# The first batch's first stage gets a program of its own

## The reference, cut to what matters

```
x  = x + quant(layernorm(x)) @ quant(ctx).T      # first block
x  = x + ffn(layernorm(x))                       # second block
ffn(h): q, k, v projections of rmsnorm(h); 16 query heads, 4 key/value heads of 128, rmsnorm of q and k, RoPE,
        causal softmax, values, output projection, residual; then rmsnorm, top 2 of 8 experts, their products, residual
```

## Time and profile before

| | |
|---|---|
| median of three runs | 1615.73 us (1614.37 to 1616.39) |
| the profiled execution's own time | 1621.27 us |
| its span in the trace | 1619.5 us |
| PE busy in the span | 1352.6 us (84%) |
| DVE, ACT, POOL busy | 766.7, 660.1, 381.9 us |
| mean granted TensorE clock | 0.93 of full speed |

### The profile page before, as it was taken

The page is one execution under the profiler, slowest core; times in us unless marked ns, Lnnn a source line. Parts: engine busy times, 40 slices in busy tenths (PEclk is TensorE's granted clock), DMA queues, the critical chain, the costliest instruction groups (busy, mean ns, idle before and its releaser), DMA issues. The chain is left out here.

```text
span 1619.5 us, 20299 instructions
## 1 busy us (share of the span) xinstructions
PE 1352.6 (84%) x6414; PEld 981.7 (61%) x6414; DVE 766.7 (47%) x2295; ACT 660.1 (41%) x2153; POOL 381.9 (24%) x558
## 2 busy tenths in 40 slices
PE   0467788899889998989999899999872599999996
PEld 0245566677667667767667777777651265665663
DVE  5626766555766555477565544554525211111110
ACT  3425664444645445465544544544520022222221
POOL 1021221213222222222223223223100123333332
PEclk9978798999989999999999999999995599999998
DMA  2223122434053131324212132330136523333332
GB/s 91 94 101 118 39 100 90 147 147 182 8 185 92 62 131 53 132 95 114 78 53 104 66 143 79 84 126 23 50 96 281 230 52 66 66 65 66 65 66 39
DMA packets 42440, 156.93 MB, mean 97 GB/s; under 512 B 5024, under 2 KB 5792, under 8 KB 33120
## 3 DMA queue, kind: packets, MB, share of 16 engines
q1 hardware_dynamic: 30624, 130.52, 21.5%
q0 software_dynamic: 10848, 24.65, 8.8%
q10 hardware_dynamic: 864, 0.46, 0.1%
HBM read 111.57 MB, written 44.04 MB: 96 GB/s over the span
## 5 line engine op out<-in xcount | busy, mean ns | idle before, releaser
L1032 DVE TENSOR_SCALAR_CACHE_REDUCE prob<-bank,nscale 128x128 f32<-128x128 f32 (+3 forms) x256 | 135.2, 547 | 296.0 <-PE bank L547 295.7
L403 POOL TENSOR_TENSOR prob<-prob,rtotal 128x128 f32<-128x128 f32 (+2 forms) x192 | 119.0, 629 | 433.9 <-DVE rtotal L1038 414.6
L760 ACT ACTIVATE pT<-bank 128x512 f32<-128x512 f32 (+3 forms) x256 | 104.5, 433 | 278.7 <-PE bank L555 278.3
L754 ACT ACTIVATE prob<-prob,bias 128x128 f32<-128x128 f32 (+3 forms) x256 | 144.9, 566 | 164.0 <-DVE prob L1032 163.0
L513 PE MATMUL bank<-w_hi,hT_hi 128*128 128x512 f32 (+1 forms) x512 | 191.9, 375 | 5.7 <-DVE rot L1006 4.3
L1396 PE MATMUL gu<-we,xT 128*128 x624 | 194.3, 465 | 2.3 <-ACT xT L1440 1.3
L384 POOL TENSOR_TENSOR r<-r,rot 128x640 f32<-128x640 f32 x64 | 103.4, 1616 | 368.0 <-DVE rot L1006 368.0
L566 PE MATMUL bank<-pT,v 128*128 128x512 f32 (+3 forms) x512 | 178.4, 451 | 1.4 <-ACT pT L760 1.4
L513 PE MATMUL bank<-w_lo,hT_hi 128*128 128x512 f32 (+1 forms) x512 | 178.4, 348 | 0.0
L513 PE MATMUL bank<-w_hi,hT_lo 128*128 128x512 f32 (+1 forms) x512 | 178.2, 348 | 0.0
L1396 PEld LDWEIGHTS gu<-we,xT 128*128 128x128 f32 x624 | 117.1, 193 | 62.1 <-issue 5.4
(11 more groups left out here) (226 smaller groups left out, 2523.5 us busy)
## 6 DMA issues: line engine op xcount, KB each, us to landing
w_hi<-ws_scratch SPq DMA_DIRECT2D x24, 1024.0 KB, 5.0
w_lo<-ws_scratch SPq DMA_DIRECT2D x24, 1024.0 KB, 7.3
we<-in_wexp SPq DMA_DIRECT2D x8, 2176.0 KB, 28.0
stage<-in_wqkvo SPq DMA_DIRECT2D x40, 256.0 KB, 6.3
ws_scratch<-w_hi SPq DMA_DIRECT2D x8, 1024.0 KB, 4.0
ws_scratch<-w_lo SPq DMA_DIRECT2D x8, 1024.0 KB, 7.0
w_hi<-ws_scratch SPq DMA_DIRECT2D x12, 512.0 KB, 6.1
w_lo<-ws_scratch SPq DMA_DIRECT2D x12, 512.0 KB, 7.0
```

The lines of the kernel that those rows point to most:

```text
L403: nc.gpsimd.tensor_tensor(p, p, rtotal[:, 4 * h + q:4 * h + q + 1].broadcast_to([P, KEYS[q]]), ALU.mult).then_inc(prob_ready, 1)
L754: nc.scalar.activation(p, p, ACT.Exp, bias=bias[:, 4 * h + q:4 * h + q + 1], scale=-1.0, accum_out=total[:, 4 * h + q:4 * h + q + 1]).then ...
L760: nc.scalar.activation(pT[:, PT_AT[j]:PT_AT[j] + QS[j]], bank[PT + j % 2][:, 0:QS[j]], ACT.Copy).then_inc(pt_copied, 1)
L1032: nc.vector.tensor_scalar(prob[h % 2][:, P_AT[q]:P_AT[q] + KEYS[q]], bank[SC + q % 2][:, 0:KEYS[q]], nscale[it % 2][:, q, h:h + 1], None, ...
```

## The change

The prologue gets its own operations; batches 1 to 3 keep theirs. Its core, with the functions added:

```
+ first_rows = [xw[0][:, :], xw[1][:, :], prob[0][:, 0:D], prob[0][:, D:2 * D]]      # four row tiles
+ amax_all, ainv_all, ascale_all: [P, TT, KC];  cmx: [NB, 1];  cmb: [NB, P]
+ FIRST_T, FIRST_P = (PT, PT + 1, AUX, PV), (0, 1, SC, SC + 1)                        # banks of transposes, of products
+ def wqkv(j, i): return aT[i] if j == 0 else w[i]                                    # group 0's q, k, v weights in aT
+ def q_bank(j, t): return bank[0] if j else bank[(0, SC)[t % 2]]
+ def kv_bank(j, t): return bank[1] if j else bank[(1, SC + 1)[t % 2]]
# DVE
+ def first_scales():            # maximum, reciprocal, two products for all four row tiles at once
+ def first_row_maxima(t): ...   # as in row_scales, into amax_all
+ def first_ctx_maxima(k):       # one 128x512 chunk of the context, waits for that chunk alone
+ def first_spread():
+     dve.wait_ge(cm_turned, 1)
+     nc.vector.tensor_reduce(cmx[:, :], bank[PV][0:NB, 0:P], AX.X, ALU.max).then_inc(cm_row, 1)
+     dve.wait_ge(cm_row, 1)
+     nc.vector.tensor_copy(cmb[:, :], cmx[:, :].broadcast_to([NB, P])).then_inc(cm_spread, 1)
+ def first_norms():             # nine steps on DVE in place of POOL's newton(0)
# PE
+ def first_maxima():
+     pe.wait_ge(camax_done, KC)
+     nc.tensor.transpose(bank[PV][0:NB, 0:P], camax[:, :], ident[:, :]).then_inc(cm_turned, 1)
+     pe.wait_ge(cm_spread, 1)
+     nc.tensor.transpose(bank[PV][:, P:P + NB], cmb[:, :], ident[0:NB, 0:NB]).then_inc(cm_back, 1)
+ def first_products():
+     for k in range(KC):
+         pe.wait_ge(cd_ready, k + 1)
+         for t in range(TT):
+             last = nc.tensor.matmul(bank[FIRST_P[t]][:, :], r[:, t, k * P:(k + 1) * P], cb[:, k, :], start=(k == 0), stop=(k == KC - 1))
# POOL
+ def add_first(t): ...          # the q part (512 wide) of add_rope(0, t); add_rope(0, t) keeps the k part (128 wide)
  tables():  + pool.wait_ge(cr_ready, KC)
- column_maxima(0)
- newton(0)
# SP
  save_x1(f): one DMA for each of four tiles, each as soon as its tile is summed (was one of 1 MB after the fourth)
  order: load_raw 0..5, save_x1(0), load_raw 6..11, load_x(1), load_ctx(1), save_qkv(0)
  (was:  load_raw 0..5, save_x1(0), load_x(1), load_ctx(1), save_qkv(0), load_raw 6..11)
```

More of the change, by code:

```diff
@@ L328, in _ @@
             save_x1(0)
+            for n in range(QKV, 2 * QKV):
+                load_raw(n)
             load_x(1)
@@ L458, in transposes_x @@
                 for k in range(KC):
-                    last = nc.tensor.transpose(bank[AUX][:, k * P:(k + 1) * P], xw[t % 2][:, k * P:(k + 1) * P], ident[:, :])
+                    last = nc.tensor.transpose(tr_bank(f, t)[:, k * P:(k + 1) * P], (xw[t % 2] if f else first_rows[t])[:, k * P:(k + 1) * P], ident[:, :])
                 last.then_inc(xt_done, 1)
@@ L668, in dequantise_rows @@
                 act.wait_ge(xr_ready, TT * f + t + 1)
+                row, back = (xw[t % 2], ascale[t % 2]) if f else (first_rows[t], ascale_all[:, t, :])
                 for k in range(KC):
                     sl = slice(k * P, (k + 1) * P)
-                    last = nc.scalar.activation(xw[t % 2][:, sl], xw[t % 2][:, sl], ACT.Copy, scale=ascale[t % 2][:, k:k + 1])
+                    last = nc.scalar.activation(row[:, sl], row[:, sl], ACT.Copy, scale=back[:, k:k + 1])
                 last.then_inc(xd_ready, 1)
@@ L736, in square_q @@
                 act.wait_ge(projq, TT * j + t + 1)
-                need(act, rope_added, TT * j + t - 1)
+                if j:
+                    act.wait_ge(rope_added, TT * j + t - 1)
+                else:
+                    need(act, first_added, t - 1)
                 for h in range(G):
-                    last = nc.scalar.activation(rot[t % 2][:, h * HD:(h + 1) * HD], bank[0][:, h * HD:(h + 1) * HD], ACT.Square,
+                    last = nc.scalar.activation(rot[t % 2][:, h * HD:(h + 1) * HD], q_bank(j, t)[:, h * HD:(h + 1) * HD], ACT.Square,
                                                 accum_out=ssum[:, t, h:h + 1])
@@ L1081, in _ @@
             sum_norm(0)
-            hidden_norm(0)
-            for c in range(RING_W, QKV):
-                lo_qkv(0, c)
+            lo_qkv(0, 3)
             for t in range(TT):
                 lo_h(0, t)
+            hidden_norm(0)
+            lo_qkv(0, 4)
+            lo_qkv(0, 5)
             dve.wait_ge(table_step, 11)
@@ L1089, in _ @@
                 rotate(0, t, False)
+                lo_qkv(1, t)
+            for t in range(TT):
                 rest_kv(0, t)
             start_norms(0)
+            first_norms()
             apply_norms(0)
@@ L1094, in _ @@
                 lo_qk(0, i)
-            for c in range(QKV):
-                lo_qkv(1, c)
+            lo_qkv(1, 4)
+            lo_qkv(1, 5)
             for it in range(NIT):
```

252 lines of the change are left out of this document (152 added, 100 removed).

## The result

The changed kernel takes 1579.95 us (median of four runs, 1578.85 to 1582.6) against 1616.06 us for the kernel before, ratio 0.978 with an interval of 0.9763 to 0.9797: 36.1 us less. Timed a second time, in five rounds on one chip, it took 1580.80 against 1617.45, ratio 0.977 (0.9754 to 0.9786). The forecast was 1575, with a range of 1567 to 1585.

The account below looks back on a forecast made before the run. Ahead of 131.5 us waits, not PE's list, were taken to set the pace; behind it PE's list does. The prologue's steps sum to -40.9 us, from 1615.7 to about 1575, range 1567 to 1585.

Parts of the forecast that it names:

- less: Rival: weight-ring loads delay the prologue, or iteration 0 pays some 6 us more for its all-reduce; 1577 to 1583, chance 0.25.
- Step A: Context scales at the program's start: column maxima without waiting for POOL's reduction, so DVE's first rounding moves from 30.65 to 20.5.
- Step B: Scaling and rounding of the context: ACT ends last, first chunk ready at 37.9, first product about 38 instead of 51.1.
- Step C: Context products and sum: sixteen matmuls take 9.0 us, statistics of the sum end at 51.2 instead of 72.2.
- D: Second norm and save of the sum: `hidden` begins at 54.2 instead of 76.8, without waiting for the save.
- G: From normalised k to iteration 0: two weight splits remain instead of six; first maxima at 90.6 instead of 131.5.
- E: Transposes after the second norm, in four banks: projections begin at 59.4 instead of 88.8, rounds take 5.2 instead of 12.0.
- Step F: Projections until k is normalised: two banks spare PE the wait for each rotation; k ready at 83.9 instead of 119.6.
- More: Rival: PE stays at full clock into iteration 0, of which 0.5 to 2.5 us passes on; 1573, chance 0.2.
- Slower: Rival: the first write to `aT` waits for late weight saves; 1625 if they land 90 us late, chance 0.02.
- My last sign of being wrong: The forecast would be wrong if first maxima to the end of attention took longer than 1092 us.

## Why the prediction was right, and where its sizes were off

**Where the bound is.** Right. What was gained lies ahead of iteration 0, and nothing behind it gives back or adds in a way that two traces of each kernel could show. The medians, 1579.95 and 1580.80, lie in the range of 1567 to 1585, but not in the band of the forecast itself (1573.5 to 1577): they lie in that of *less* (1577 to 1583), whose mechanism did not occur.

**Step A.** 20.5 forecast, 19.05 measured. Of the 1.45, 0.8 is luck: the input landed earlier, so the norm stood ready at 11.5 and not at 12.2. The four unknown operations with their waits and `ctx_scales` took 1.7 us (17.37 to 19.05, with the first transpose hidden beside the last maximum), 1.8 estimated; but 18.2 and 1.8 make 20.0, and I had written 20.5. The price that I read there as the worth of PE's maxima was that of the all-reduce's place.

**Step B.** ACT ends last, as said, so the step is counted from ACT's start: 18.3 us to the first product (17.42 to 35.72), 19.7 forecast. DVE's rounding is off the path by the slack I had named: in the variant with the all-reduce behind the tables ACT hid 1.8 us of its delay (2.5 named).

**Step C is the mis-sized term.** I took "x8" in the earlier trace rows as eight matmuls; it is four, since each product of 128x512 in f32 stands in the trace as two instructions, and the block shows x32 for sixteen. Read rightly, a first row tile at 5.32 and three at 3.70 give 16.4, where the block measured 15.9; the forecast's 9.0 us held half the work. PE's last product was to end at 46.9 and ended at 51.6, 4.7 late: 6.9 of the term, less the 2.2 that steps A and B were early. The last statistics were 3.2 late (54.4 for 51.2), since DVE's tail behind PE was 2.8 and not 4.3: in a block twice as long, the first bank is complete earlier before its end. And PE, not the arrival of the chunks, is the limit of this stretch.

**Steps D to G.** From there the distances are those of the forecast, with the forecast's in brackets: C to D 3.0 (3.0), D to E 4.2 (5.2), E to F 24.5 (24.5), F to G 6.7 (6.7). Step F holds inside as well: the first rotation comes 5.6 us after the first projection (5.6), q of tile 2 7.1 (7.0), the last q matmul 12.6 (12.7). Taken away again, three parts cost what was expected for them: transposes 6.0, splits 4.45, Newton 1.5. Two did not: the save 0.6 for 1.5, the second banks 18.6 for 12. From the first projection to the first maxima the change gained 11.6 us (42.75 before, 31.20 now), less than the banks alone cost when removed; so these prices hold in the new order and do not add up to the gain.

**The median.** The landmarks give 38.7 and 39.4 us, the medians 36.1 and 36.7. The forecast's own sum, 40.9, was 2.2 over the first of the landmarks: 3.2 late at C, and 1.0 back between D and E. The intervals of the two ratios stand for gains of 32.8 to 38.3 us and 34.6 to 39.8. The other 2 to 3 us are smaller than what the stretch behind the prologue does by itself (6.7 us between two executions of one kernel), but they came out alike in both timings. Whether a part of it belongs to the change stays open: the mean of that stretch is 1092.1 in two traces of before and 1093.3 in twelve with a changed prologue, which two traces can't decide.

**Rivals.** *More* needed PE to stay at full clock into iteration 0. The granted clock there was 1.00 (92.8 to 97 us), where before had 0.50 in its like stretch (131.5 to 136). PE's timeline:

```profile
93.37 0.41 PE L590 MATMUL bank<-kT_hi,qT_hi 128*128 128x384 f32 x1 [1.65 <-DVE prob L1119]
```

It waited 1.65 us here instead of 7.40, and this matmul took 0.41 instead of 0.66. But iteration 0 was as long as before to 0.04 us. That fits the all-reduce holding what follows; yet iteration 0 of before was itself 1.0 us shorter in its second trace, so a gain under 1 us would not be seen. *Less* did not happen: `stage` never held ACT between the squares. *Slower* was far off; its 1625 was also a slip, since saves that land 90 us late would give 1665 by its own rule. My last sign of being wrong, a stretch longer than 1092 us, was drawn from a window cut 2.9 us too early, and with 6.7 us of variation it could not have told anything: the second trace of the changed kernel has 1095.1.

## What to carry to other kernels

Where each engine waits for the tile before, give a prologue its own buffers and PSUM banks, and look at the order with them: one bank each for q and for k and v took 30.2 us in the kernel before, where the two alternated, and 42.4 with all q tiles first, against 23.9 with two banks each. A third of the last difference was clock: with waits of 2.7 us ahead of the q tiles the granted clock was 0.74, with two banks 0.93. Count instructions in a trace against those in the kernel before pricing them: x8 was four matmuls here. Before replacing a slow operation on another engine, move it to the front of that engine's list: an all-reduce that held DVE 10 us cost nothing once it stood ahead of independent work. And measure such a change at a landmark of the trace, since here the rest of the program varied by 6.7 us, more than most of the effects that were asked about.

## What was not expected of the hardware

- Two executions of one program differ by 6.7 us in some 1092 us of attention. For the same 5060 matmul instructions PE was busy 971.3 us at a mean clock of 0.94 in one and 962.0 at 0.95 in the other, while DVE, ACT and POOL differ by 0.6 at most. It is not that alone: over the fourteen traces the length does not follow PE's busy time (1090.8 us at 968.4 busy, 1095.0 at 965.4).
- The same 32 matmul instructions in the same order took 15.57 to 16.91 us in nine traces, by when their pace doubled, while the clock in the windows read 1.00 throughout.
- Each all-reduce of the kernel before comes with two instructions on POOL's sequencer that change its configuration, eight for four calls, and each call has its own wait of 5.81 to 6.37 us. With the all-reduce first in POOL's list the first such instruction stands at 1.0 us, and the call ran 0.14 us behind its input. By the view of line 374:

```profile
L374 POOLq MODIFY_POOL_CONFIG  x8: 11/11/16, 23.5 to 694.2; - x8
L374 POOL PARTITION_ALL_REDUCE camaxall<-camax x4: 391/392/392, 29.4 to 700.4; - x4
```

- POOL's addition took longer on less data, in POOL's timelines of the changed kernel and of the kernel before:

```profile
70.85 1.73 POOL L410 TENSOR_TENSOR r<-r,rot 128x512 f32<-128x512 f32 x1 [0.42 <-DVE rot L1084]
```

```profile
102.16 1.58 POOL L384 TENSOR_TENSOR r<-r,rot 128x640 f32<-128x640 f32 x1 [4.06 <-DVE rot L1006]
```

That DVE works beside it is not the reason: in the changed kernel DVE is idle from 71.4 to 72.9 beside this row, and busy nearly all along beside that at 77.09, which took 1.72. The 60 additions of 128x640 in the same trace have a median of 1.57. What makes the narrower one slower stays open.
